# Order of two ScalarE jobs in the chunk steps of a graph layer: copy of a turned pick, rectification of a chunk

## The reference, cut to what matters

```
h   = relu(layernorm(x))
m   = relu(concat(h[src], edge_attr_16) @ w1a + b1a)      # per edge, 48 -> 96
s   = segment_sum(m @ w1b + b1b, dst) / max(count, 1)     # per node
x   = x + relu(concat(h, s) @ w2a + b2a) @ w2b + b2b
# second layer: relu(h2[src] + edge_attr_32), summed per dst, added to (1+eps)*h2
```

## Time and profile before

| what | us |
|---|---|
| median of 3 runs | 7443.95 |
| the three runs | 7443.95, 7433.59, 7458.75 |
| span of the profiled execution, first to last instruction | 7360.0 |
| the profiled execution's own time | its span and what lies around it; none is listed apart from the three runs |
| median less span | 83.95 |
| TensorE's mean granted clock over the span | 0.917 |

### The profile page before, as it was taken

One profiled execution on the slowest core, in us unless ns is written; L12 is line 12 of the kernel. 1 busy time (PEld: TensorE's weight loads), 2 busy tenths in 40 slices (PEclk: granted clock), 3 DMA queues, 4 the chain that ended last, 5 costly groups with the idle time before them and its releaser, 6 DMA issues. The chain is left out here.

```text
span 7360.0 us, 107042 instructions
## 1 busy us (share of the span) xinstructions
PE 6429.2 (87%) x32834; PEld 5436.7 (74%) x32835; DVE 3791.4 (52%) x9052; ACT 4370.5 (59%) x8707; POOL 4564.4 (62%) x4834
## 2 busy tenths in 40 slices
PE   7888888888888888888887888888888889888888
PEld 5777777777777777777777777777777777777777
DVE  5343434434444443434446666666666666666666
ACT  5555555555555555555556666666666666666665
POOL 5666666666666666666655666666666666666665
PEclk8999899888898999898998999999999999999999
DMA  3222221222222122222211111111111111111111
GB/s 104 55 55 55 54 54 54 55 55 55 55 56 54 54 55 55 54 54 57 56 44 43 42 44 44 44 39 44 44 42 41 44 44 42 41 44 44 44 39 40
DMA packets 331462, 367.43 MB, mean 50 GB/s; under 512 B 87161, under 2 KB 256536, under 8 KB 331166
## 3 DMA queue, kind: packets, MB, share of 16 engines
q0 software_dynamic: 152000, 160.05, 10.0%
q1 hardware_dynamic: 46276, 130.67, 5.3%
q10 hardware_dynamic: 133146, 76.25, 3.7%
HBM read 358.17 MB, written 8.46 MB: 50 GB/s over the span
## 5 line engine op out<-in xcount | busy, mean ns | idle before, releaser
L1015 PE MATMUL bank<-part_high,owner_hot 125*128 125x448 f32 (+1 forms) x10500 | 4250.6, 405 | 224.1 <-issue 162.9
L1015 PE MATMUL bank<-part_low,owner_hot 125*128 125x448 f32 (+1 forms) x10500 | 4127.5, 393 | 152.6 <-issue 150.9
L986 POOL DMA_INDIRECT gathered<-projected_rows,indices x2500 | 2366.8, 947 | 1412.8 <-issue 705.7
L986 POOL DMA_INDIRECT gathered<-hidden_rows,indices x2250 | 2135.2, 949 | 1277.1 <-issue 854.6
L1015 PEld LDWEIGHTS bank<-part_high,owner_hot 125*128 125x128 f32 x10500 | 2144.2, 204 | 505.2 <-issue 228.8
L1015 PEld LDWEIGHTS bank<-part_low,owner_hot 125*128 125x128 f32 x10500 | 2137.9, 204 | 412.6 <-issue 189.7
L1118 ACT ACTIVATE owner_hot<-owner_in,minus_piece 125x256 fp32r<-125x256 f32 (+2 forms) x3948 | 1591.4, 484 | 128.4 <-remote 69.9
L1261 DVE SCALAR_TENSOR_TENSOR hidden<-window_f,places_now,bank 128x512 f32<-128x512 f32 x1500 | 1104.8, 737 | 1074.6 <-remote 609.0
L1123 ACT ACTIVATE owner_hot<-owner_hot 125x1792 fp32r<-125x1792 f32 (+1 forms) x750 | 1275.5, 1701 | 23.8
L1317 DVE TENSOR_TENSOR sums<-sums,bank 97x48 f32 (+1 forms) x1250 | 244.2, 195 | 1694.6 <-remote 1396.7
L1045 PEld LDWEIGHTS bank<-hidden,messages 128*97 128x97 f32 x6250 | 644.4, 170 | 424.2 <-issue 418.3
(11 more groups left out here) (128 smaller groups left out, 2721.4 us busy)
## 6 DMA issues: line engine op xcount, KB each, us to landing
owner_in<-owner_rows SPq DMA_DIRECT2D x188, 448.0 KB
edges<-in_edge ACTq DMA_DIRECT2D x124, 400.0 KB
gathered<-projected_rows,indices POOLq DMA_INDIRECT x2500
gathered<-hidden_rows,indices POOLq DMA_INDIRECT x2250
hidden<-owner_rows SPq DMA_DIRECT2D x62, 448.0 KB
edges<-in_edge ACTq DMA_DIRECT2D x124, 200.0 KB
projected_rows<-projected SPq DMA_DIRECT2D x25, 168.0 KB
sources<-in_src_cols SPq DMA_DIRECT2D x1, 1562.5 KB, 6.4
```

What stands on the lines that cost most here:

```text
L986: pool.indirect_dma_start(gathered_rows(k, row)[:, t, :], None, table, bass.IndirectOffsetOnAxis(ap=index(k, odd(turn))[:, t:t + 1], axis= ...
L1015: last = nc.tensor.matmul(bank[pick_home[home]][:, 0:PITCH * D].rearrange("p (f b) -> p f b", b=PITCH)[:, :, 0:rows.shape[2]], pick_hot(pi ...
```

## The change

On ScalarE, `copy_pick` of two chunks ahead (and its wait for `picks_turned`) moves ahead of `rectify` of the present chunk; in step 0 the DMA of `load_edges` stays behind `rectify` and so is behind the copy too. `make_hots` stays last. On TensorE, `edge_products` gets a wait for `rectified` of the chunk that last used the same bank: for slots 0 and 1 that is two chunks back, for slots 3 and 4 three, for slot 2 five. `chunks` serves both layers, but layer 1 has no `copy_pick` and no `edge_products`, so its lists stay as they are.

```
@@ edge_products
                         pe.wait_ge(picks_copied, picks_before(turn) + (picks_of(k, turn)[0] + ROUND + 1))
+                        pe.wait_ge(rectified, chunks_before(turn) + (k + SLOTS + 1 - since(edge_home, k)))
                         nc.tensor.matmul(bank[edge_home[k]][:, 0:TILES * H1], edge_t(k, odd(turn)),
@@ chunks (ScalarE)
                         for k in range(SLOTS):
-                            rectify(k, turn)
-                            if k == 0 and not last:
-                                load_edges(step_on(turn, 1))
                             if layer == 0 and not (last and k + 2 >= SLOTS):
                                 later, slot = at(turn, k + 2)
                                 for n in picks_of(slot, later):
                                     copy_pick(n, later)
+                            rectify(k, turn)
+                            if k == 0 and not last:
+                                load_edges(step_on(turn, 1))
```

## The result

| kernel | median, us | runs from to, us |
|---|---|---|
| before | 7447.64 | 7433.59 to 7458.75 |
| after | 7505.96 | 7505.23 to 7519.99 |

The medians lie 58 us apart, 0.8%; the ratio on record is 1.009 (95% interval 1.0077 to 1.0102). The change costs time, and the forecast was 100 us.

What follows compares the result with a forecast made beforehand. GpSimd's gathers and pauses were taken to bound layer 0. Late starts of 1.2 us a turn, less 0.4 coming back, gave 0.8 x 125 = +100 us on 7444: 7544 us, range 7400 to 7660.

Steps and rivals of the forecast that it cites:

- The rule that was weighed: Take the engine of highest occupancy, here TensorE, and start sooner what it waits for; by that the change helps.
- chunks 1, 2 and 4: in time: Layer 0's first gathers of these chunks would start no later, since they had room; costed at nothing.
- chunk 3 as the one that pays: Chunk 3's first gather would start late by a mean 1.16 us a turn; chunk 0's by 0.05.
- What comes back: A delay ahead of chunk 3 shortens GpSimd's later pause by 0.79 us; half taken, 0.4 us a turn.
- 84 us above the span: Median 7443.95 us against profiled span 7360.0; taken as time around the span and carried over to the forecast.
- 2.63 us of lateness: Chunk 3's gathers, second turn: copy's start 2045.58 + 1.25 = 2046.83 against a recorded start of 2044.20.
- two neighbouring turns: GpSimd's timeline in layer 0: runs of 12 and 8 gathers, a pause behind each, taken as the beat.
- The terms at nothing: Costed at zero: earlier copy, later scatter, `make_hots`, SP's load and edge load, and TensorE's added wait (173 us uncovered).
- Swallowed: Rival: GpSimd's 3.25 us pause after chunk 3's late start absorbs the delay; 7444 us, within 22; chance 0.15.
- TensorE gains: Rival: `edge_products` waits less for the copy and GpSimd's pauses shorten; 7360 us, or 7402 for half; chance 0.20.
- A third pause: Rival: chunk 3's gathers wait out a full pause, old pauses stay; 7714 us, or 7579 in half the turns; chance 0.18.

Runs made afterwards that it cites:

- the further profile: One more profile of the unchanged kernel, taken on a chip where it measured 7462.92 us; the profiled execution took 7467.12 us.
- split_psum_first_2: Kernel before, copy moved between picked tile's rectification and the fetched tiles' (L1143, L1144 here); no added TensorE wait: 7477.36 us, 1.0066, where before takes 7433.92.
- split_rows_late: Kernel before, fetched tiles rectified first, freeing gathers; then copy, picked tile's rectification and a 384-element filler releasing scatter and TensorE, which gets an added wait: 7440.96 us, 1.0015.
- gathers_wait_copy: Kernel before, ScalarE's order kept; only GpSimd's gathers also wait for the copy of the pick two chunks ahead: 7363.86 us, 1.0018, where before takes 7349.58.
- pe_wait_alone: Kernel before with only TensorE's added wait ahead of the edge products: 7349.44 us, ratio 1.0001, where before takes 7349.58.
- the earlier trace: The first profile of the unchanged kernel, on which the prediction was based; its span is 7360.0 us.
- split_psum_first: Kernel before, copy moved between the picked tile's rectification and the fetched tiles'; no added TensorE wait: 7368.33 us, 1.0023, where before takes 7349.58.
- Without pacing: Kernel before without GpSimd's two pacing waits of layer 0, for `halves_summed` and `pieces_summed`: 7975.84 us, ratio 1.0728, where before takes 7431.01.

## Why the prediction was right, and where not

**The bound** was read rightly. Layer 0 moves as GpSimd's gathers and pauses do, with TensorE busier. The rule that was weighed (the Trainium skill, Perfetto Trace Analysis, Identifying the Most-Contended Engine) names TensorE. This case disagrees: TensorE's waits for the copy did not shrink but grew, from 259.5 us (162.9 + 96.6) in the further profile to 333.5 us (250.8 + 82.7) after, and delaying TensorE without holding the gathers cost 0.15%.

**The mechanism** was right: the gathers wait for the rectification, which waits for the turned pick (shown by split_psum_first_2, some four fifths of the cost, against split_rows_late; on the quick chip by gathers_wait_copy, where nothing but that wait was added).

**The step that failed** is "chunks 1, 2 and 4: in time", and with it chunk 3 as the one that pays. The lateness was the copy's recorded start plus 1.25 us, held against the recorded start of the gathers. That takes the copy's start as given. But the forecast itself had read that TensorE's increments come 4 us and more late while GpSimd gathers, and of the copies that come late most start in a pause of GpSimd (180 of 220 in after). The change moves the pauses, and such copies move with them. Measured, per turn: late by 2.4 us, not 1.2; 1.75 us given back, not 0.4; chunk 3 on time. The net is 0.51 us where 0.8 was forecast. Both terms were too small, one by half and one by three quarters, and their errors offset each other: that the sum came so near is luck.

Chunk 3 was not picked without ground, though. On the quick chip pe_wait_alone keeps the beat of the earlier trace rows (94 of 122 turns pause for over 1 us at the third gather of chunk 0, 94 at chunk 3's), and there split_psum_first pauses as long at chunk 3's first gather in 39 turns and at chunk 4's in 26, where pe_wait_alone does in 4 and 2. In the changed kernel's own trace, with the looser beat, chunk 3 is on time.

**What comes back** was named, but its size and the reason for its size failed. A pause at a first gather stands in for most of the pause at the next third gathers: 1.75 of 2.38 us after, and in split_psum_first against pe_wait_alone 1.19 of 1.36 us (first gathers 1.71 against 0.35, third gathers 3.48 against 4.67). The forecast let it shorten that pause by only 0.79 us, in half of the turns, because the pauses "follow the end of the gathers, not TensorE's work". These pauses got shorter when the run ahead of them was broken.

**The base.** The "84 us above the span" is not what lies around it. The changed kernel's profiled execution took 7519.99 us with a span of 7517.9 us: 2.1 us. The rest was a quicker execution than the timed ones. It did no harm to the sum, since the cost was added to the median. The lateness was read from it too, and there the beat is evener than in the further profile (0.31 us a turn ahead of first gathers, not 0.88), so that two turns seemed to stand for all. The second of the two does not even show the pattern that "two neighbouring turns" were said to show. Behind the 0.63 us ahead of chunk 3's first gather at 2044.20 stand these two:

```profile
2047.10 0.94 POOL L986 DMA_INDIRECT gathered<-projected_rows,indices  x1 [1.96 <-issue]
2049.29 0.94 POOL L986 DMA_INDIRECT gathered<-projected_rows,indices  x1 [1.25 <-remote]
```

The run of twelve is broken there, and the copy of 2045.58, from which the 2.63 us of lateness were read, starts inside that pause.

**The terms at nothing.** TensorE's wait as an instruction: nothing, shown (1.0001). Its lateness behind the copy: no more than split_rows_late's 0.15% (0.06 to 0.24), which also has the filler. TensorE did wait 164.3 us for L1144 in after, without a price of its own that could be told apart. Later `make_hots`, SP's load and the load of the edges weren't changed one by one. In split_rows_late `make_hots` starts later still than in the change, and all of it together is that 0.15%. Whether the last fifth of the change's cost is anything but noise stays open.

**The rivals.** *Swallowed* is out: the interval lies 0.77% and more above. *TensorE gains* is out, by the waits above. *A third pause* has its mechanism in single waits: the longest are full pauses of 4 us. But the "against" written beside it decided: most of the next pause falls away, so it costs half a microsecond and not two.

## What to carry to other kernels

Before an instruction is put behind a wait, ask which engine's buffers it frees, and whether that engine's own running holds back the event waited for. If it does, the delay can be a full stop and no slip. A recorded start time may be used as a fixed bound only if what sets it isn't moved by the change. And a wait that guards no data may still be worth its idle time: take it out and measure before calling it lost.

## What the runs showed of the hardware

While GpSimd issues gathers back to back, some of TensorE's increments are seen late: the copy above started 7.7 us after the recorded end of the only thing it waited for, 2.2 us after the gathers stopped, and 220 of the 547 copies counted there were over 1 us late. Others were not: of the 318 copies of that stretch for which ScalarE stood idle and whose turn ended during a run of gathers, a quarter started within 0.04 us. Without pacing the gathers' own wait reached 9.69 us and layer 0's mean granted clock stood at 0.84, where it is 0.91 in the profiles of before and after; TensorE was busy 2806 us of the stretch, not 2968 (its stage's row, columns as above):

```profile
300.00:3700.00 3400.00, 2805.67 (x13242) 2211.68 (x13240) 1201.34 (x2744) 1659.18 (x3822) 1854.24 (x1963) 0.84 0.20 48
```

In that run TensorE itself creeps at times, not its increments alone. These are matmuls of one scatter, about 2 us apart and with no recorded wait, while GpSimd gathers up to 2008.84:

```profile
2004.77 0.24 PE L1046 MATMUL bank<-hidden,messages 128*97 128x48 f32 x1 [0.88 <-issue]
2006.91 0.24 PE L1046 MATMUL bank<-hidden,messages 128*97 128x48 f32 x1 [1.90 <-issue]
2009.02 0.24 PE L1046 MATMUL bank<-hidden,messages 128*97 128x48 f32 x1 [1.88 <-issue]
```

What holds TensorE and its increments back is not shown.

The same program took 7349.58, 7431.01, 7433.92 and 7462.92 us on four chips, and layer 1's turn, which no kernel here touches, 27.64 us in the further profile and 3200 x 18 / 2117 = 27.21 us in the one of the earlier trace rows, by its row for layer 1:

```profile
4100.00:7300.00 3200.00, 2842.92 (x14445) 2482.98 (x14445) 2003.02 (x4934) 2034.08 (x3405) 2005.54 (x2117) 0.93 0.17 43
```

The cost of L1143 behind the copy was 0.23% on the first and 0.66% on the third. Each chip was used in one session, so chip and session can't be told apart. Why the times differ, and why the quicker chip pays less, stays open.
